# Gated attention: the weighing of the values as three split products

## The chip, the cores and the metric

One core of one Trainium2 chip. The metric is the device time in microseconds of one launch of the whole program, here the median of three runs. Engines: PE (TensorE, matrix products), ACT (ScalarE), DVE (VectorE), POOL (GpSimd), SP (SyncE, issues most transfers).

## The reference

A small transformer of two blocks on 16 sequences of 548 tokens (36 image patches and 512 text tokens) with 128 channels. The change touches one part, the gated attention of the first block, cut here to what matters:

```python
h = x * jax.lax.rsqrt(ms + EPS) * norm_scale
uv = jax.nn.silu(h @ W1 + b1)
u, v, base = jnp.split(uv, [256, 512], axis=-1)
q, k = (base[:, :, None, :] * gamma + beta)[:, :, 0], (...)[:, :, 1]
qk = jnp.einsum('bnd,bmd->bnm', q, k) / 128
qk = _rope(qk)                       # rotates pairs along the m axis
kernel = jnp.square(jax.nn.relu(qk))
out = u * jnp.einsum('bnm,bme->bne', kernel, v)
return out @ W2 + b2 + shortcut
```

The remaining stages (router and experts, spiking attention, last feed-forward) stay as they are. All is float32.

## The kernel before

`gated_attention` works batch by batch (16), tokens in two halves of 274 columns. The inner product with the values sums over 548 keys: two times two tiles of 128, and a tail. It is cut into five units of work, g = 0 to 4: units 0 and 1 are the first half of the queries, 3 and 4 the second, with two of the four 128-key tiles in each, and unit 2 (`TAIL_UNIT`) holds the key tails of both halves.

A unit passes through four engines: PE `score` (products of q and k into PSUM), DVE `rotate` (L704, L705: times cos and sin), POOL `add` (L661, L662, for the tail L659), ACT `kernel_of` (Relu L590, Square L598), PE `weigh` (L509, for the tails L490), which sums over units in the PSUM tile `kv`. After unit 2 and unit 4 DVE's `gate` (L737) multiplies `kv` by u. `down` (L469) is the product with W2 for the batch before, `residual` (L742) adds it to H. Beside that each engine prepares the next batch: POOL `keep_hn` (L635: the rounded tokens) and `make` (L648: q and k), DVE `tokens_low` (L710), `low_of` (L716, L719, L720) and `bias_v` (L728), ACT `base_out`, `u_out`, `v_out` (L563, L569, L576), PE `project_base`, `project_u`, `project_v`.

The scores and the projections are already split products: `split_matmul` multiplies rounded parts (type float32r) and remainders in three matmuls, rounded by rounded, rounded by remainder and remainder by rounded. POOL makes the rounded part, DVE the remainder by a subtraction. `weigh` and `down` use plain float32 matmuls.

The order on each engine is written out by hand in its `units` function, with semaphores between the engines; a queue runs strictly in that order. The tiles of a unit (scores, by_cos, by_sin, rot, kern) have two copies, so unit g waits for unit g - 2 in them. Batch b + 1 is prepared during batch b: on PE, the order in the steady loop is score 2, v tail, weigh 0, score 3, base, weigh 1, down, score 4, weigh 2, u 0, weigh 3, v, score 0 of the next batch, weigh 4, score 1 of the next, u 1.

Of the kernel before, what the change touches and what calls it, by code (L numbers as in the profile page):

```python
# [9 lines left out]
ALU = mybir.AluOpType  # L10
# [331 lines left out]
def gated_attention(nc, k, x, H, HN, moe_d):  # L342
# [7 lines left out]
    with ExitStack() as st:  # L350
# [4 lines left out]
        sin = sb("sin", [P, 3, 2, S])  # L355

        GAP = 32
        hs = [[sb(f"hs{p}{part}", [P, 2, HALF], F32R) for part in range(2)] for p in range(2)]
# [9 lines left out]
        v = [sb(f"v{p}", [P, 5, EXPAND]) for p in range(2)]  # L368
# [18 lines left out]
        v_biased = sem("v_biased")  # L387
# [31 lines left out]
        def _(sp):  # L419
            sp.dma_start(cos[:], x["cos"]).then_inc(tables_in, 16)  # L420
            sp.dma_start(sin[:], x["sin"]).then_inc(tables_in, 16)
# [3 lines left out]
            w = NROWS // 4  # L425
            for sums in (y_d[0], y_d[1]):
                yv = sums.rearrange("(p r) d -> p (r d)", p=P)
                for c in range(4):
                    sp.dma_start(yv[:, c * w:(c + 1) * w], zeros[:]).then_inc(filled, 16)
            sp.dma_start(rows_d[NT:NROWS, :].rearrange("(p r) d -> p (r d)", p=64), zeros[0:64, 0:(NROWS - NT) * ROWW // 64]).then_inc(filled, 16)  # L430
            sp.dma_start(slots_d, x["empty_slots"]).then_inc(filled, 16)
            sp.wait_ge(filled, 16 * 10)

        @block.tensor
        def _(pe):
# [52 lines left out]
            def weigh_tail(p, j):  # L488
                for e in range(2):
                    last = nc.tensor.matmul(kv[:, e, 0:HALF], v[p][0:TAILS, 4, e * P:(e + 1) * P], kern_tail[p][0:TAILS, j, :],  # L490
# [3 lines left out]
            def weigh(b, p, g, first=False):  # L494
                pe.wait_ge(kern_done, UNITS * b + g + 1)
                if g == 0:
                    pe.wait_ge(v_sb, 2 * b + 1)
                    if not first:
                        pe.wait_ge(gated, 2 * b)
                if g == TAIL_UNIT:  # L500
                    pe.wait_ge(v_sb, 2 * b + 2)
                    last = weigh_tail(p, 0)
                else:
                    j, mt = unit(g)
                    if g == TAIL_UNIT + 1:
                        pe.wait_ge(gated, 2 * b + 1)
                    for e in range(2):
                        for side in range(2):
                            last = nc.tensor.matmul(kv[:, e, 0:HALF], v[p][:, mt + 2 * side, e * P:(e + 1) * P],  # L509
                                                    kern[(p + g) % 2][:, side, :], start=mt == 0 and side == 0, stop=False)  # L510
# [3 lines left out]

            def units(b, p, first=False, final=False):
                for g in range(UNITS):
                    if g < 3:
                        score(b, p, g + 2)
                    if g == 0:
                        project_v(b, p, True)  # L520
                    if g == 1 and not final:
                        pe.wait_ge(v_biased, 2 * b + 2)
                        project_base(b + 1, 1 - p)
                    weigh(b, p, g, first)
                    if g == 3 and not final:
                        project_v(b + 1, 1 - p, False)
                    if g >= 3 and not final:
                        score(b + 1, 1 - p, g - 3)
                    if g == 1 and not first:
                        if final:  # L530
                            pe.wait_ge(v_biased, 2 * b + 2)
                        else:
                            pe.wait_ge(base_sb, b + 2)
                        down(b - 1)
                    if g == 2 and not final:
                        if not first:
                            pe.wait_ge(resid, b)
# [2590 lines left out]
```

## Time and profile before

| | us |
|---|---|
| median of 3 runs (1675.97 to 1676.25) | 1676.23 |
| the profiled execution: time | 1674.66 |
| the profiled execution: span | 1672.8 |
| of it the gated attention | about 95 to 458 |
| mean granted clock of TensorE | 0.896 |

| engine | busy us (share of the span) |
|---|---|
| PE | 1300.5 (78%) |
| PE, weight loads | 915.5 (55%) |
| DVE | 1036.9 (62%) |
| ACT | 789.4 (47%) |
| POOL | 875.4 (52%) |

Busy shares are averages over stages with different limits. The stretch from 95 to 458 us is the one that the change touches, and it has to be read on its own. Times in the timeline are microseconds from the start of the span. A matmul's record is longer than the distance to the next one, since matmuls are pipelined: what a group of them costs is the distance between starts. A plain float32 matmul shows as two records. "x8" means eight records merged in one row.

### The profile page before, as it was taken

To read this page: it belongs to the slowest core of one execution; us is meant where nothing else is said; L and a number is where in the kernel's file an instruction comes from. 1 tells how busy PE (TensorE), PEld (TensorE's weight loads), DVE (VectorE), ACT (ScalarE), POOL (GpSimd) and SP (SyncE) were. 2 spreads that over 40 slices of the span, in tenths; PEclk is the share of its full clock that TensorE was granted. 3 is DMA by queue.
4 is the path that set the end of the run, shared out by engine and by line. 5 is a ranking of instruction groups with operands and counts; after the bars stand their busy time and mean duration, and the time that the engine had idled before them with its cause. 6 is when DMAs were issued, how large, how long until landed. Compare 5 with 4: busy or idle time off the path is not lost. (4 is left out here: it accounts for less than half of the span.)

```text
span 1672.8 us, 27218 instructions
## 1 busy us (share of the span) xinstructions
PE 1300.5 (78%) x8667; PEld 915.5 (55%) x8667; DVE 1036.9 (62%) x1943; ACT 789.4 (47%) x1420; POOL 875.4 (52%) x880
## 2 busy tenths in 40 slices
PE   5679999999883430676672883888889888999997
PEld 3567777777652320565561562333333357877775
DVE  2766666666557774211111588888888566667786
ACT  2225454555353330232220454878777657665443
POOL 1455555555331003688885524776776045735766
PEclk8879999999995565899995786999999999999999
DMA  5052000000001031344445200000000311333443
GB/s 181 1 208 114 0 0 0 0 0 0 0 0 28 0 108 28 88 93 83 80 73 154 81 1 2 2 1 0 0 0 1 113 50 55 94 95 46 56 61 40
DMA packets 84627, 81.05 MB, mean 48 GB/s; under 512 B 18330, under 2 KB 73203, under 8 KB 83147
## 3 DMA queue, kind: packets, MB, share of 16 engines
q1 hardware_dynamic: 56205, 59.43, 11.4%
q0 software_dynamic: 26176, 19.40, 8.2%
q10 hardware_dynamic: 2160, 1.13, 0.2%
q8 instruction: 47, 0.77, 0.2%
q14 instruction: 39, 0.31, 0.1%
HBM read 46.36 MB, written 39.64 MB: 51 GB/s over the span
## 5 line engine op out<-in xcount | busy, mean ns | idle before, releaser
L1969 PE MATMUL at_slot<-at_qm,at_ks 128*128 128x512 bf16 (+1 forms) x640 | 160.1, 383 | 19.3 <-DVE at_clip L2174 9.9
L2838 POOL DMA_INDIRECT out_h<-ff_tokens x70 | 109.0, 1557 | 74.7 <-DVE ff_tokens L2891 56.9
L509 PE MATMUL ga_kv<-ga_kern,ga_v 128*128 128x274 f32 x512 | 132.3, 400 | 14.3 <-ACT ga_kern L598 12.8
L2053 ACT ACTIVATE at_clip<-at_slot,at_four 128x1024 bf16<-128x1024 f32 (+1 forms) x96 | 106.8, 1112 | 31.9 <-PE at_slot L1969 30.1
L1452 POOL DMA_INDIRECT moe_sums<-ex_y,slot_sums x69 | 108.3, 1570 | 22.1 <-issue 20.9
L2174 DVE TENSOR_SCALAR at_clip<-at_slot 128x1024 bf16<-128x1024 f32 (+1 forms) x96 | 116.1, 1218 | 3.0 <-PE at_slot L1969 2.6
L509 PEld LDWEIGHTS ga_kv<-ga_kern,ga_v 128*128 128x128 f32 x512 | 92.3, 189 | 37.8 <-ACT ga_kern L598 20.4
L661 POOL TENSOR_TENSOR ga_rot<-ga_by_cos,ga_by_sin 128x274 f32<-128x274 f32 x64 | 48.4, 756 | 114.2 <-DVE ga_by_sin L705 114.1
L590 ACT ACTIVATE ga_rot<-ga_rot 128x274 f32<-128x274 f32 x128 | 55.1, 432 | 109.0 <-POOL ga_rot L661 96.9
L1542 DVE TENSOR_SCALAR ex_share<-ex_rows,owner_sb 128x1 f32<-128x1 f32 x31 | 6.6, 214 | 148.4 <-PE ex_ps_y L1494 148.4
L2828 POOL DMA_INDIRECT by_group<-mx_stage,mx_place_i x69 | 72.0, 1044 | 50.0 <-ACT mx_stage L2714 29.2
L1969 PEld LDWEIGHTS at_slot<-at_qm,at_ks 128*128 128x128 bf16 (+1 forms) x640 | 40.0, 97 | 93.6 <-issue 81.6
L1493 PE MATMUL ex_ps_y<-ex_down,ex_hid 128*128 128x128 f32 (+1 forms) x600 | 86.9, 295 | 3.9 <-ACT ex_hid L1524 3.8
L1436 POOL DMA_INDIRECT ex_rows<-token_rows,slot_tokens x69 | 67.2, 974 | 39.5 <-issue 20.4
L1524 ACT ACTIVATE ex_hid<-ex_ps_up,cols_sb 128x274 f32<-128x274 f32 (+1 forms) x96 | 43.3, 488 | 91.9 <-PE ex_ps_up L1480 91.8
L2110 POOL TENSOR_SCALAR at_qm<-at_qs,at_headmask 128x548 bf16<-128x548 bf16 x120 | 86.3, 738 | 0.0
L1493 PEld LDWEIGHTS ex_ps_y<-ex_down,ex_hid 128*128 128x128 f32 (+1 forms) x600 | 80.6, 204 | 8.2 <-ACT ex_hid L1524 7.0
L1378 POOL DMA_INDIRECT expert_slots<-ct_ids,ct_row x20 | 19.7, 983 | 120.6 <-DVEq L1277 116.0
L2891 DVE SCALAR_TENSOR_TENSOR ff_tokens<-mx_e,ff_tokens 128x128 f32<-128x128 f32 x210 | 72.0, 349 | 15.8 <-ACT ff_tokens L2775 10.8
L2102 POOL TENSOR_SCALAR sa_qkv<-sa_qkv 128x548 f32<-128x548 f32 x48 | 44.5, 927 | 66.5 <-ACT sa_qkv L2065 66.5
L2053 ACT ACTIVATE down_b<-at_slot,at_four 128x1024 bf16<-128x1024 f32 (+1 forms) x48 | 53.4, 1113 | 17.2 <-PE at_slot L1969 16.4
L1518 ACT ACTIVATE ex_xt<-ex_ps_xt 128x256 f32<-128x256 f32 (+1 forms) x32 | 12.7, 396 | 100.6 <-PE ex_ps_xt L1470 100.6
(480 smaller groups left out, 3918.8 us busy)
## 6 DMA issues: line engine op xcount, KB each, us to landing
moe_sums<-ga_zeros SPq DMA_DIRECT2D x8, 1152.0 KB, 13.4
ar_rows<-moe_sums SPq DMA_DIRECT2D x34, 256.0 KB, 3.8
ex_down<-in_down SPq DMA_DIRECT2D x32, 192.0 KB, 2.6
by_group<-in_blank SPq DMA_DIRECT2D x1, 4655.0 KB, 19.8
ff_tokens<-by_group SPq DMA_DIRECT2D x17, 266.0 KB, 3.4
token_rows<-ct_rows SPq DMA_DIRECT2D x17, 256.0 KB, 2.4
out_h<-mx_rows SPq DMA_DIRECT2D x22, 192.0 KB, 2.1
H<-in_text SPq DMA_DIRECT2D x1, 4096.0 KB, 22.1
```

The source lines that it names most:

```text
L509: last = nc.tensor.matmul(kv[:, e, 0:HALF], v[p][:, mt + 2 * side, e * P:(e + 1) * P], kern[(p + g) % 2][:, side, :], start=mt == 0 and si ...
L590: last = nc.scalar.activation(r[:, side], r[:, side], ACT.Relu)
L1436: nc.gpsimd.indirect_dma_start(out=rows[t % NR][:], out_offset=None, in_=rows_d, in_offset=bass.IndirectOffsetOnAxis(ap=gather_idx[:, t:t ...
L1452: nc.gpsimd.indirect_dma_start(out=sums, out_offset=bass.IndirectOffsetOnAxis(ap=scatter_idx[:, t:t + 1], axis=0), in_=y[t % YR][:], in_of ...
L1493: nc.tensor.matmul(out, hid[e % 2][0:m, f, at:at + P], down[e % 2][0:m, f, :], start=opens and f == 0, stop=False)
L1969: last = nc.tensor.matmul(to[r0:r0 + r, g % 2, :].rearrange("p (s n) -> p s n", s=2), ks[m][:, t * P:t * P + r], qm[m][:, 2 * g:2 * g + 2, ...
L2053: nc.scalar.activation(to[0:r], of[0:r], ACT.Relu, bias=four[0:r], scale=-1.0).then_inc(by_act, 1)
L2110: return eng.tensor_scalar(qm[m][:, h, :], qs[:], headmask[:, h:h + 1], 1.0, ALU.mult, ALU.mult)
L2174: nc.vector.tensor_scalar(to[0:r], of[0:r], 4.0, None, ALU.min).then_inc(by_dve, 1)
L2828: nc.gpsimd.indirect_dma_start(out=grouped_d, out_offset=bass.IndirectOffsetOnAxis(ap=place_i[:, t:t + 1], axis=0), in_=stage[:, t, :], in ...
L2838: nc.gpsimd.indirect_dma_start(out=out, out_offset=bass.IndirectOffsetOnAxis(ap=ids, axis=0), in_=R[j % RING], in_offset=None, bounds_chec ...
L2891: nc.vector.scalar_tensor_tensor(r, part(e), share(e), r, ALU.mult, ALU.add).then_inc(acc if e < 3 else weighed, 1)
```

## The change

Kernel and values are each split into a rounded part and a remainder. `v_out` writes its Silu over `v_pre`; POOL rounds it (`round_v`), DVE takes the remainder (`values_low`). ACT squares a unit twice: once into the rounded part of the kernel, once in full precision over `rot`; the remainder is a subtraction, on DVE for units 0 and 4 and on POOL for units 1 and 3 (`kern_low`). PE's `weigh` becomes `weigh_high` (the products with the rounded kernel) and `weigh_low` (those with its remainder), and other groups of products stand between the two in PE's order. In unit 0 the product with the values' remainder is also in `weigh_low`. The tails stay plain float32 and get their own `weigh_tails`. `rot` is now free after the subtraction that reads it.

To make room in SBUF, the zeros from which the expert buffers are filled are a quarter of the width and are sent in 16 transfers per buffer instead of 4, the sine table's tail is a tile of its own, and `ukv` of one half lies over W1.

```diff
-        v = [sb(f"v{p}", [P, 5, EXPAND]) for p in range(2)]
+        v_parts = [[sb(f"v{p}{part}", [P, 4, EXPAND], F32R) for part in range(2)] for p in range(2)]
+        v_tail = [sb(f"v_tail{p}", [2 * GAP, EXPAND]) for p in range(2)]
...
-        kern = [sb(f"kern{p}", [P, 2, HALF]) for p in range(2)]
+        kern_parts = [[sb(f"kern{p}{part}", [P, 2, HALF], F32R) for part in range(2)] for p in range(2)]
...
-        zeros = sb("zeros", [P, NROWS // 4])
+        zeros = sb("zeros", [P, NROWS // 16])
...
-        ukv = [sb(f"ukv{j}", [P, 2, HALF]) for j in range(2)]
+        ukv = [k["W1"][:, 0:S].rearrange("p (e n) -> p e n", e=2), sb("ukv", [P, 2, HALF])]
...
+            def products(p, g, v_part, kern_part, start):
+                j, mt = unit(g)
+                for e in range(2):
+                    for side in range(2):
+                        last = nc.tensor.matmul(kv[:, e, 0:HALF], v_parts[p][v_part][:, mt + 2 * side, e * P:(e + 1) * P],
+                                                kern_parts[(p + g) % 2][kern_part][:, side, :], start=start and side == 0, stop=False)
+                return last
+
+            def weigh_high(b, p, g, first=False):
+                pe.wait_ge(kern_done, UNITS * b + g + 1)
+                if g == 0:
+                    pe.wait_ge(v_rounded, b + 1)
+                    if not first:
+                        pe.wait_ge(gated, 2 * b)
+                if g == TAIL_UNIT + 1:
+                    pe.wait_ge(gated, 2 * b + 1)
+                products(p, g, 0, 0, g in (0, TAIL_UNIT + 1))
+                if g > 0:
+                    products(p, g, 1, 0, False)
+
+            def weigh_low(b, p, g):
+                if g in (0, UNITS - 1):
+                    pe.wait_ge(low_by_dve, 2 * b + 1 + (g > 0))
                 else:
+                    pe.wait_ge(low_by_pool, 2 * b + 1 + (g > 1))
+                last = products(p, g, 0, 1, False)
+                if g == 0:
+                    pe.wait_ge(v_low, b + 1)
+                    last = products(p, g, 1, 0, False)
                 if g == UNITS - 1:
                     last = weigh_tail(p, 1)
                 last.then_inc(kv_done, 1)
...
+                score(b, p, 2)
+                project_v(b, p, True)
+                weigh_high(b, p, 0, first)
+                score(b, p, 3)
+                weigh_low(b, p, 0)
+                pe.wait_ge(v_biased, 2 * b + 2)
+                if not final:
+                    project_base(b + 1, 1 - p)
+                weigh_high(b, p, 1)
+                if not first:
+                    if not final:
+                        pe.wait_ge(base_sb, b + 2)
+                    down(b - 1)
+                weigh_low(b, p, 1)
+                score(b, p, 4)
+                weigh_tails(b, p)
+                if not final:
+                    if not first:
+                        pe.wait_ge(resid, b)
+                    project_u(b + 1, 1 - p, 0)
+                weigh_high(b, p, 3)
+                if not final:
+                    project_v(b + 1, 1 - p, False)
+                weigh_low(b, p, 3)
+                if not final:
+                    score(b + 1, 1 - p, 0)
+                weigh_high(b, p, 4)
+                if not final:
+                    score(b + 1, 1 - p, 1)
+                weigh_low(b, p, 4)
+                if not final:
+                    project_u(b + 1, 1 - p, 1)
...
-                    last = nc.scalar.activation(kern[(p + g) % 2][:], r[:], ACT.Square)
-                last.then_inc(kern_done, 1)
+                    nc.scalar.activation(kern_parts[(p + g) % 2][0][:], r[:], ACT.Square).then_inc(kern_done, 1)
+                    nc.scalar.activation(r[:], r[:], ACT.Square).then_inc(squared, 1)
...
+            def kern_low(b, p, g):
+                pool.wait_ge(squared, 4 * b + g - (g > TAIL_UNIT) + 1)
+                high, low = kern_parts[(p + g) % 2]
+                nc.gpsimd.tensor_tensor(low[:], rot[(p + g) % 2][:], high[:], ALU.subtract).then_inc(low_by_pool, 1)
+
+            def round_v(b, p, first=False):
+                pool.wait_ge(v_sb, 2 * b + 1)
+                if not first:
+                    pool.wait_ge(kv_done, UNITS * b - UNITS)
+                pool.sem_inc(met, 1)
+                nc.gpsimd.tensor_copy(v_parts[p][0][:], v_pre[:]).then_inc(v_rounded, 1)
+
             def units(b, p, first=False, final=False):
                 for g in range(UNITS):
+                    if g in (1, 3):
+                        kern_low(b, p, g)
                     if g < UNITS - 1:
                         add(b, p, g + 1, first and g == 0)
                     elif not final:
                         add(b + 1, 1 - p, 0)
+                        round_v(b + 1, 1 - p, first)
...
+            def values_low(b, p):
+                dve.wait_ge(v_rounded, b + 1)
+                nc.vector.tensor_tensor(v_parts[p][1][:], v_pre[:], v_parts[p][0][:], ALU.subtract).then_inc(v_low, 1)
...
                     if g == 0:
+                        kern_low(b, p, 0)
+                        values_low(b, p)
                         bias_v(b, True, first)
+                    if g == 4:
+                        kern_low(b, p, 4)
```

## Rows read from the trace of the kernel before

**Rows 1.** Busy time by stretch: us, PE, PEld, DVE, ACT, POOL, PEclk, DMA, GB/s

```profile
196.00:238.00 42.00, 40.55 (x219) 33.03 (x219) 28.62 (x42) 21.41 (x38) 22.10 (x31) 1.00 0.00 0
```

**Rows 2.** The page's 40 slices: granted clock of PE in tenths of full speed

```profile
PEclk8879999999995565899995786999999999999999
```

**Rows 3.** Timeline, DVE, first gate of batches 0, 6, 7, 15: start, us, engine, line

```profile
122.58 0.73 DVE L737 TENSOR_TENSOR ga_ukv<-ga_kv,ga_u 128x548 f32<-128x548 f32 x1 [2.75 <-PE ga_kv L490]
...
252.70 0.73 DVE L737 TENSOR_TENSOR ga_ukv<-ga_kv,ga_u 128x548 f32<-128x548 f32 x1 [0.98 <-PE ga_kv L490]
...
274.26 0.73 DVE L737 TENSOR_TENSOR ga_ukv<-ga_kv,ga_u 128x548 f32<-128x548 f32 x1 [0.97 <-PE ga_kv L490]
...
446.09 0.73 DVE L737 TENSOR_TENSOR ga_ukv<-ga_kv,ga_u 128x548 f32<-128x548 f32 x1 [1.08 <-PE ga_kv L490]
```

**Rows 4.** Timeline, PE, batch 6

```profile
240.96 0.30 PE L92 MATMUL ga_scores<-ga_q,ga_k 128*128 128x274 f32 x1
241.09 0.30 PE L93 MATMUL ga_scores<-ga_q,ga_k 128*128 128x274 f32 x1
...
246.92 2.01 PE L509 MATMUL ga_kv<-ga_kern,ga_v 128*128 128x274 f32 x8
248.77 2.01 PE L469 MATMUL ga_misc<-ga_ukv,W_sb 128*128 128x274 f32 x8
...
251.47 1.19 PE L490 MATMUL ga_kv<-ga_kern_tail,ga_v 50*128 50x274 f32 x4
...
258.74 2.12 PE L509 MATMUL ga_kv<-ga_kern,ga_v 128*128 128x274 f32 x8 [0.63 <-ACT ga_kern L598]
```

**Rows 5.** Timeline, DVE, batch 6

```profile
240.46 0.73 DVE L737 TENSOR_TENSOR ga_ukv<-ga_kv,ga_u 128x548 f32<-128x548 f32 x1 [2.35 <-PE ga_kv L490]
241.53 0.73 DVE L704 TENSOR_TENSOR ga_by_cos<-ga_scores,ga_cos 128x548 f32<-128x548 f32 x1 [0.34 <-PE ga_scores L93]
...
245.15 0.73 DVE L710 TENSOR_TENSOR ga_hs<-HN,ga_hs 128x548 fp32r<-128x548 f32 x1 [1.17 <-POOL ga_hs_tail L636]
245.80 0.19 DVE L711 TENSOR_TENSOR ga_hs_tail<-HN,ga_hs_tail 128x36 fp32r<-128x36 f32 x1
245.90 0.71 DVE L698 TENSOR_TENSOR ga_by_cos<-ga_scores,ga_cos 64x548 f32<-64x548 f32 x1
...
253.35 1.15 DVE L716 TENSOR_TENSOR ga_q<-ga_q 128x548 fp32r<-128x548 f32 x1
254.42 0.71 DVE L704 TENSOR_TENSOR ga_by_cos<-ga_scores,ga_cos 128x548 f32<-128x548 f32 x1
...
255.69 0.68 DVE L719 TENSOR_TENSOR ga_k<-ga_k 128x512 fp32r<-128x512 f32 x1
256.29 0.66 DVE L720 TENSOR_TENSOR ga_k_tail<-ga_k,ga_k_tail 128x36 fp32r<-128x36 f32 x1
```

**Rows 6.** Timeline, POOL, batch 6

```profile
244.21 0.64 POOL L635 CAST ga_hs<-HN 128x548 fp32r x1
...
248.22 1.34 POOL L659 TENSOR_TENSOR ga_rot<-ga_by_cos,ga_by_sin 64x548 f32<-64x548 f32 x1 [3.21 <-issue]
...
251.09 0.67 POOL L661 TENSOR_TENSOR ga_rot<-ga_by_cos,ga_by_sin 128x274 f32<-128x274 f32 x1
...
253.91 0.83 POOL L648 TENSOR_SCALAR ga_k_tail<-ga_base,cols_sb 128x36 fp32r<-128x36 f32 x1
255.86 1.04 POOL L661 TENSOR_TENSOR ga_rot<-ga_by_cos,ga_by_sin 128x274 f32<-128x274 f32 x1 [1.11 <-DVE ga_by_sin L705]
```

**Rows 7.** Timeline, ACT, batch 6

```profile
240.13 0.66 ACT L598 ACTIVATE ga_kern<-ga_rot 128x548 f32<-128x548 f32 x1
240.70 1.04 ACT L576 ACTIVATE ga_v<-ga_v_pre 128x1024 f32<-128x1024 f32 x1
242.19 0.72 ACT L569 ACTIVATE ga_u<-ga_misc,cols_sb 128x548 f32<-128x548 f32 x1 [0.45 <-PE ga_misc L93]
```

**Rows 8.** Timeline, PE, unit 4 of the last batch

```profile
450.68 2.12 PE L509 MATMUL ga_kv<-ga_kern,ga_v 128*128 128x274 f32 x8 [1.62 <-ACT ga_kern L598]
```

More of the change, by code:

```diff
@@ L354, in gated_attention @@
         cos = sb("cos", [P, 3, S])
[L355 removed]
+        sin = sb("sin", [P, 2, 2, S])
         GAP = 32
+        sin_tail = sb("sin_tail", [2 * GAP, S])
         hs = [[sb(f"hs{p}{part}", [P, 2, HALF], F32R) for part in range(2)] for p in range(2)]
@@ L513, in weigh, with weigh_tails @@
                 last.then_inc(kv_done, 1)
+            def weigh_tails(b, p):
+                pe.wait_ge(kern_done, UNITS * b + TAIL_UNIT + 1)
+                pe.wait_ge(v_sb, 2 * b + 2)
+                weigh_tail(p, 0).then_inc(kv_done, 1)
             def units(b, p, first=False, final=False):
[L516 to L537, printed above, removed]
-                        project_u(b + 1, 1 - p, 0)
-                    if g == 4 and not final:
-                        project_u(b + 1, 1 - p, 1)
@@ L653, in add @@
                 pool.wait_ge(rot_done, n + 1)
-                if not first:
+                if g == 0 and not first:
+                    pool.wait_ge(low_by_pool, 2 * b)
+                if g == 1 and not first:
+                    pool.wait_ge(low_by_dve, 2 * b)
+                if g == 3:
+                    pool.wait_ge(low_by_pool, 2 * b + 1)
+                if g == 2:
+                    pool.wait_ge(low_by_dve, 2 * b + 1)
+                if g == 4:
                     pool.wait_ge(kern_done, n - 1)
@@ L680, in _ @@
             add(0, 0, 0, True)
+            round_v(0, 0, True)
             units(0, 0, first=True)
@@ L698, in rotate @@
                     nc.vector.tensor_tensor(by_cos[par][0:2 * GAP], xs[0:2 * GAP], halves(cos[0:2 * GAP, 2, :]), ALU.mult)
-                    nc.vector.tensor_tensor(by_sin[par][high], xs[low], halves(sin[low, 2, 0, :]), ALU.mult)
-                    nc.vector.tensor_tensor(by_sin[par][low], xs[high], halves(sin[high, 2, 1, :]), ALU.mult).then_inc(rot_done, 1)
+                    nc.vector.tensor_tensor(by_sin[par][high], xs[low], halves(sin_tail[low]), ALU.mult)
+                    nc.vector.tensor_tensor(by_sin[par][low], xs[high], halves(sin_tail[high]), ALU.mult).then_inc(rot_done, 1)
                 else:
@@ L724, in bias_v @@
                 dve.wait_ge(v_ps, 2 * b + tails + 1)
-                if not first:
+                if tails and not first:
                     dve.wait_ge(v_sb, 2 * b)
@@ L737, in gate, with kern_low @@
                 nc.vector.tensor_tensor(ukv[j][:], kv[:, :, 0:HALF], u[p][:, :, j, :], ALU.mult).then_inc(gated, 1)
+            def kern_low(b, p, g):
+                dve.wait_ge(squared, 4 * b + g - (g > TAIL_UNIT) + 1)
+                high, low = kern_parts[(p + g) % 2]
+                nc.vector.tensor_tensor(low[:], rot[(p + g) % 2][:], high[:], ALU.subtract).then_inc(low_by_dve, 1)
+            def values_low(b, p):
+                dve.wait_ge(v_rounded, b + 1)
+                nc.vector.tensor_tensor(v_parts[p][1][:], v_pre[:], v_parts[p][0][:], ALU.subtract).then_inc(v_low, 1)
             def residual(b):
```

41 lines of the change are left out of this document (17 added, 24 removed).

## The prediction, made before the changed kernel had run

> **What bounds the kernel now.** I read the busy times by stretch first [rows 1]. In 42 us of the gated attention PE is busy 40.55 us at a granted clock of 1.00, DVE 28.62 and POOL 22.10. That says PE, but a busy sum hides pipelining, so I went to the timeline. The gate of a batch's first half starts at 252.70 and again at 274.26 [rows 3]: one batch takes 21.56 us, and the attention is 16 of these.
>
> PE's own order comes next [rows 4]. Split products (fp32r) are issued every 0.13 us (240.96, 241.09), a score's six take 0.76 us, and 0.31 us after the last slot (241.22) DVE starts on them (241.53 [rows 5]). A plain f32 weigh unit of four products holds PE from 246.92 to 248.77, 1.85 us. The tail's two hold it from 251.47 until their gate starts at 252.70, 1.23 us, with 0.08 in front 1.31. One real stall stands in the batch: weigh unit 4 starts at 258.74, 0.63 us late, released by ACT's Square. So the kernel is bound by PE, with the chain gate, low_of, rotate 4, add 4, Square just behind it.
>
> Last, the other three engines [rows 5 to 7], because the change puts all its new work there. What the reader is to see is who waits for whom between DVE and POOL. A DVE subtraction with both inputs in SBUF takes 0.73 us when POOL is idle (245.15, 548 columns), but 1.15 at 253.35, beside POOL's tensor_scalars. The 36-column L720 takes 0.66 at 256.29 against 0.19 for its twin L711. POOL's add takes 1.04 at 255.86 instead of 0.67: 256.90 less 0.67 is 256.23, just 0.54 after L719 began. POOL's 36-column k_tail takes 0.83. So these instructions run one after the other, not side by side, and a waiting one gets its turn between two instructions of the other engine. DVE instructions that read PSUM show no such stretch: L704 at 254.42 takes 0.71 beside k_tail, 0.73 at 241.53 with POOL idle.
>
> **The change part by part.** PE: per batch 16 plain products (4 units of 1.85 us, 7.40 us) become 48 split ones of 0.127 us, 6.10 us: 1.3 us less. The tails stay. The stall at unit 4 and small gaps are the most that could go on top.
>
> ACT: a second Square per unit, 4 per batch. A Square holds ACT 0.57 us (240.13 to 240.70 [rows 7]), 2.3 us more on an engine that is half idle; it matters because v_out and u_out queue behind it.
>
> POOL gets kern_low of units 1 and 3 and round_v. A 548-column tensor_tensor is 1.34 us (L659 [rows 6]), a cast of 548 columns 0.64, so 1024 columns about 1.20: 3.9 us. DVE gets kern_low of units 0 and 4 and values_low. L719's 512 columns held the pair 0.54 us, so 548 columns 0.57 and 1024 columns 1.07: 2.2 us, and by the rows above these are lost to POOL too wherever it has work.
>
> Other edits at nothing: the zero fill as 32 transfers of a quarter of the size on SP's queue, whose last wait comes at the end of a block with over 300 us of cover, and costs SP alone without it; the tables as four transfers and the smaller memset, behind which DVE waits for PE's first scores anyway; the aliased ukv and sin_tail, with the same instructions as before.
>
> The new waits: round_v waits for v_out (ACT), and behind it in POOL's queue stand add 1, keep_hn and all later work, for which ACT and PE wait. values_low waits for round_v, and behind it on DVE stand bias_v of the tail, tokens_low and rotate 2, for which PE's base projection, score 4 and POOL wait. PE's low products wait for kern_low, and v's projection and the next scores stand behind them. So I laid one batch out, each engine's queue in program order, with durations from the rows. Time 0 is where the previous batch's second gate starts (240.46 in the trace of now).
>
> Rotate 0 of the new batch ends at -3.1. kern_low 4 of the old batch (DVE) and add 0 (POOL, two halves, 1.28) meet, and add 0 ends at -1.2, 0.57 later than alone. From the end of an add to a high product PE needs 1.21 us now (add 4 ends 0.63 after 256.90, PE starts at 258.74), of which the Square is 0.66, so Square starts 0.50 after an add. ACT: two Squares and v_out (1.04), to 1.5. POOL: round_v to 2.7. DVE: gate to 0.65, rotate 1 to 2.0, kern_low 0, held by round_v, 2.7 to 3.3. POOL's add 1 has its first half to 3.9; DVE's values_low to 5.0; the second half to 5.6; keep_hn to 6.4. DVE: tokens_low 6.5 to 7.2, rotate 2. That one and its handover take 2.32 us (245.90 to add 2 at 248.22), so POOL's add 2 starts at 9.6 (now 7.8) and ends at 10.9. Up to here 1.8 us are lost.
>
> From there POOL: make q 1.54, to 12.4; add 3, to 13.7. ACT: 0.50, two Squares, u_out 0 (0.72), to 16.1; PE projects v (12 products, 1.43) to 17.6. In parallel POOL: make k (1.54) with low_of q let in between, to 15.8, k_tail 16.1, kern_low 3 to 17.4; then DVE's low_of k, in turn with add 4, to 18.6. PE's next score 0 waits for that: 18.7 to 19.5; rotate 0 begins 0.31 later and takes 1.36, to 21.1. It ended at -3.1 one batch earlier: 24.2 us a batch. By the other branch: add 4 17.9 to 19.2, high products from 20.4, 1.02, the score 0.76, low products 0.51, tail 1.31: 24.0. I take 24.0, since every contest was charged in full.
>
> Sum: from the first batch's first gate to the last's are 446.09 - 122.58 = 323.5 us, 15 x 21.57 [rows 3]. 15 x (24.0 - 21.57) = 36.5 us. The first batch pays round_v and its follow-up once more, about 1.5 us. The last has no next batch to feed, and its unit 4, 1.62 us late by Square at 450.68 [rows 8], can hide its own low part: 0. Together 38 us. The profiled execution took 1674.7 us with a span of 1672.8, 1.5 below the median of 1676.2; by the span the new profile shows 1711, and the median becomes 1714.
>
> What the trace of before does not show is the new DVE work beside POOL. Its bounds are 0 (as for DVE's instructions on PSUM) and its full hold plus the wait. I take the latter: these have the form of L716 and L719 (f32 less fp32r into fp32r), the nearest rows. With 0 the path is: v_out to 1.1, round_v 2.3, add 1 3.6, keep_hn 4.4, tokens_low and rotate 2, add 2 from 7.5, add 3 to 11.65; Squares and u_out 2.4, v 1.43, low products 0.51, score 0, 0.31 and rotate 0 2.4, to 18.45: 21.5 us a batch.
>
> The Trainium skill, SBUF — State Buffer, section "SBUF: two separate sides", has this as a rule that speaks against the change: VectorE instructions with two SBUF inputs and GpSimd instructions that read SBUF take one port pair as an exclusive lock for the whole instruction, and the loser fully blocks. By the rule the result is the 24 us batch, without it the 21.5 us one. The trace agrees with it in the stretched instructions [rows 5 and 6].
>
> **The rivals.** (A) PE sets the batch, which gets shorter. For: PE is the busiest now. From the tails' start to the high products of unit 4 are 7.3 us now, at least 6.9 with add 4 not stretched; then PE needs 3.6 us to the end of the tail and 9.15 back to the tails (seven groups of six 0.76 or less, high and low products 3.1, down 1.85, base in them): 19.7 to 20.0 us, and 15 x (19.85 - 21.57) = -26 gives 1650 us. It decides if v_out, round_v and kern_low 3 find slack in POOL's queue. Against: even without contention POOL's path is 21.5. (B) The path through POOL and ACT binds, but its contests are absorbed: 21.5 us a batch, 1677 us. Against: the 1.04 and 1.15 us rows. (C) Between: one or two contests fall into idle time (kern_low 4 after add 0, low_of k before kern_low 3): 22.1 to 23.3 us a batch, 1685 to 1704 us. (D) Worse: PE's longer idle stretches cost it granted clock, which is 9 tenths or more of full in the attention's slices but 5 or 6 tenths in slices of other stages [rows 2]; 25 us a batch or more, 1730 and up. (E) The new products are not single passes: the scores' products of the same shape and type run at 0.127 us, so this gets nothing of its own.
>
> **How the numbers follow.** Forecast (23.3 to 24.8 us a batch, 1704 to 1727): 0.50. C: 0.20. D: 0.08. B: 0.10, 0.06 of it within the bound and 0.04 above it. A: 0.12. That makes faster 0.12, same 0.06, slower 0.82, at a bound of 0.2% (3.4 us), about what a measurement of this kernel can tell from no change. The range leaves out A and D, together 0.20: from B's 1677 to the forecast's 1727.
>
> **What would show it.** First gates 24 us apart (A: 20, B: 21.5). PE well under 40.55 us busy in 42. The new 548-column subtractions on DVE at 1.0 us or more in the mean against 0.73 alone, POOL's adds well above 0.67. PE idle before the base projection (released by tokens_low), before score 0 (by low_of k), before the high products of units 0 and 4. Add 2 some 9.6 us after the second gate. I am wrong if PE idles under 1 us per batch, or if the new subtractions keep to 0.73 us beside a busy POOL.

## The result and the profile after

The changed kernel takes 1729.7 us (median of 4, 1726.67 to 1729.99) against 1676.1 us: ratio 1.0316, 95% interval 1.0298 to 1.0334. It is slower, as forecast, by 53.6 us where 38 were forecast, and 2.7 us beyond the end of the range. The profiled execution took 1730.0 us with a span of 1728.2.

The first gates again, DVE's timeline of the changed kernel, batches 0, 5, 6 and 15 (of before: rows 3):

```profile
124.70 0.73 DVE L791 TENSOR_TENSOR W_sb<-ga_kv,ga_u 128x548 f32<-128x548 f32 x1 [2.76 <-PE ga_kv L496]
...
249.32 0.73 DVE L791 TENSOR_TENSOR W_sb<-ga_kv,ga_u 128x548 f32<-128x548 f32 x1 [1.50 <-PE ga_kv L496]
...
274.17 0.73 DVE L791 TENSOR_TENSOR W_sb<-ga_kv,ga_u 128x548 f32<-128x548 f32 x1 [1.47 <-PE ga_kv L496]
...
497.40 0.73 DVE L791 TENSOR_TENSOR W_sb<-ga_kv,ga_u 128x548 f32<-128x548 f32 x1 [1.87 <-PE ga_kv L496]
```

A batch takes 274.17 - 249.32 = 24.85 us. The fifteen distances are 497.40 - 124.70 = 372.7 us against 323.5: 49.2 of the 55.4 us by which the span grew. The first gate comes 2.1 us later, the last batch takes 1.4 us more from its first gate to its residual (497.40 to 509.64 against 446.09 to 456.95), and 2.7 us lie behind the attention.

Busy time by stretch, changed kernel (columns as in rows 1):

```profile
196.00:238.00 42.00, 34.77 (x218) 29.25 (x217) 30.91 (x40) 22.53 (x40) 27.50 (x33) 1.00 0.00 0
...
498.00:502.00 4.00, 2.51 (x13) 2.22 (x13) 1.41 (x3) 1.59 (x5) 2.66 (x3) 0.63 0.00 0
502.00:506.00 4.00, 4.00 (x15) 3.58 (x16) 0.73 (x1) 0.49 (x1) 0.00 (x0) 0.52 0.00 0
```

PE is busy 34.77 us in 42 where it was 40.55, at full clock; DVE has 2.3 and POOL 5.4 us more. No engine is full: the batch is a chain. From the first gate on, only the last batch shows a lower granted clock, 0.50 from 499 to about 506 us, the lower of the two levels (1.2 of 2.4 GHz). PE in that batch:

```profile
498.28 2.50 PE L504 MATMUL ga_kv<-ga_kern,ga_v 128*128 128x274 f32 x12 [0.91 <-DVE W_sb L791]
501.99 3.11 PE L504 MATMUL ga_kv<-ga_kern,ga_v 128*128 128x274 f32 x12 [1.21 <-ACT ga_kern L628]
505.03 1.57 PE L496 MATMUL ga_kv<-ga_kern_tail,ga_v_tail 50*128 50x274 f32 x4
```

The twelve products of unit 4 take 3.0 us (501.99 to 505.03), where twelve at 0.127 us take 1.5. What made the clock fall is not shown: PE had waited 0.91 us just before, and in the kernel before it waited 0.91 and 1.62 us in the last batch (446.97, and 450.68 in rows 8) and kept 1.00.

Who waits, from the waits of the changed kernel between 130 and 480 us, some 14 batches (waiting instruction, releaser, us in total, times, longest):

```profile
PE ga_misc L91 <- DVE ga_hs_tail L765: 19.7, 14, 1.4
PE ga_scores L91 <- DVE ga_k_tail L774: 18.0, 15, 1.2
PE ga_misc L91 <- ACT ga_u L599: 12.1, 14, 0.9
PE ga_kv L504 <- DVE ga_kern L796: 5.6, 14, 0.4
```

PE waits 1.4 us a batch for tokens_low before the base projection, 1.2 for low_of k before score 0, 0.9 for u_out before the values' tail, and 0.4 for kern_low 4 before the low products of unit 4. The first two places are those of the prediction; the other two it did not have, and the wait before the high products of unit 4 that it had is not there. PE from score 0 on, in the same batch:

```profile
255.00 0.39 PE L91 MATMUL ga_scores<-ga_q,ga_k 128*128 128x274 f32 x1 [1.21 <-DVE ga_k_tail L774]
...
255.86 1.18 PE L504 MATMUL ga_kv<-ga_kern,ga_v 128*128 128x274 f32 x8
256.87 0.29 PE L91 MATMUL ga_scores<-ga_q,ga_k 128*128 128x274 f32 x1
...
258.21 0.79 PE L504 MATMUL ga_kv<-ga_kern,ga_v 128*128 128x274 f32 x4 [0.42 <-DVE ga_kern L796]
```

Now DVE and POOL around them, one batch:

```profile
251.91 2.85 DVE L773 TENSOR_TENSOR ga_k<-ga_k 128x512 fp32r<-128x512 f32 x1
254.68 0.18 DVE L774 TENSOR_TENSOR ga_k_tail<-ga_k,ga_k_tail 128x36 fp32r<-128x36 f32 x1
...
257.44 0.72 DVE L796 TENSOR_TENSOR ga_kern<-ga_rot,ga_kern 128x548 fp32r<-128x548 f32 x1
260.15 0.73 DVE L791 TENSOR_TENSOR ga_ukv<-ga_kv,ga_u 128x548 f32<-128x548 f32 x1 [2.00 <-PE ga_kv L496]
...
262.07 0.72 DVE L796 TENSOR_TENSOR ga_kern<-ga_rot,ga_kern 128x548 fp32r<-128x548 f32 x1
263.72 1.68 DVE L800 TENSOR_TENSOR ga_v<-ga_v_pre,ga_v 128x1024 fp32r<-128x1024 f32 x1 [0.93 <-POOL ga_v L712]
```

```profile
251.59 1.36 POOL L705 TENSOR_TENSOR ga_kern<-ga_rot,ga_kern 128x548 fp32r<-128x548 f32 x1
252.92 0.66 POOL L699 TENSOR_TENSOR ga_rot<-ga_by_cos,ga_by_sin 128x274 f32<-128x274 f32 x1
253.54 0.66 POOL L700 TENSOR_TENSOR ga_rot<-ga_by_cos,ga_by_sin 128x274 f32<-128x274 f32 x1
257.60 1.09 POOL L699 TENSOR_TENSOR ga_rot<-ga_by_cos,ga_by_sin 128x274 f32<-128x274 f32 x1 [3.39 <-DVE ga_by_sin L759]
...
262.25 1.44 POOL L712 CAST ga_v<-ga_v_pre 128x1024 fp32r<-128x1024 f32 x1 [2.94 <-ACT ga_v_pre L604]
263.65 0.67 POOL L699 TENSOR_TENSOR ga_rot<-ga_by_cos,ga_by_sin 128x274 f32<-128x274 f32 x1
264.28 1.65 POOL L700 TENSOR_TENSOR ga_rot<-ga_by_cos,ga_by_sin 128x274 f32<-128x274 f32 x1
...
269.88 1.34 POOL L697 TENSOR_TENSOR ga_rot<-ga_by_cos,ga_by_sin 64x548 f32<-64x548 f32 x1 [0.80 <-DVE ga_by_sin L754]
```

Three meetings are to be seen. At 257.44 kern_low 4 runs 0.72 us undisturbed and add 0 waits for it, 1.09 instead of 0.66. At 263.72 values_low waits for the first half of add 1, runs, and the second half takes 1.65. And low_of k (L773, 512 columns, 0.68 us in rows 5) takes 2.85 us: it starts to wait in kern_low 3 and is let in only when POOL's queue is empty, behind kern_low 3 and both halves of add 4 (254.16).

### The profile page after: what moved, and what is told of

It is laid out like the page before. It is cut to its first block and busy times, and to the rows that moved or that the text cites. A ratio compares the mean times of both kernels' runs of the same rounds, so it can differ in the third digit from the quotient of the medians.

```text
span 1728.2 us, 28002 instructions
## 1 busy us (share of the span) xinstructions
PE 1297.9 (75%) x8923; PEld 927.7 (54%) x8923; DVE 1100.1 (64%) x1991; ACT 821.2 (48%) x1484; POOL 957.7 (55%) x928
## 5 line engine op out<-in xcount | busy, mean ns | idle before, releaser
L2036 PE MATMUL at_slot<-at_qm,at_ks 128*128 128x512 bf16 (+1 forms) x640 | 160.4, 384 | 19.6 <-DVE at_clip L2241 10.0
L504 PEld LDWEIGHTS ga_kv<-ga_kern,ga_v 128*128 128x128 f32 x768 | 108.2, 194 | 33.5 <-ACT ga_kern L628 10.4
L1445 POOL DMA_INDIRECT expert_slots<-ct_ids,ct_row x20 | 19.7, 984 | 120.7 <-DVEq L1344 116.2
```

The lines of the kernel that those rows point to most:

```text
L504: last = nc.tensor.matmul(kv[:, e, 0:HALF], v_parts[p][v_part][:, mt + 2 * side, e * P:(e + 1) * P], kern_parts[(p + g) % 2][kern_part][:, ...
L2036: last = nc.tensor.matmul(to[r0:r0 + r, g % 2, :].rearrange("p (s n) -> p s n", s=2), ks[m][:, t * P:t * P + r], qm[m][:, 2 * g:2 * g + 2, ...
```

## The experiments

All versions start from the changed kernel unless said otherwise. "Batch" is the distance of first gates, last less first, over 15. The ratios are to the kernel before on the same chip. The chip of e1 to e4 took 1759.2 us for the kernel before, where the others took 1675 to 1676, so for these four the batch is the number to compare. The kernel before has no trace on that chip: its 21.57 us are those of the first one.

| run | batch, us | total, us | ratio to before (interval) |
|---|---|---|---|
| before | 21.57 | 1676.1 | 1 |
| changed | 24.85 | 1729.7 | 1.0316 (1.0298 to 1.0334) |
| e1 PE's work only | 21.03 | 1753.8 | 0.9974 (0.9960 to 0.9988) |
| e2 no subtraction on DVE | 23.03 | 1784.3 | 1.0140 (1.0117 to 1.0163) |
| e3 values rounded by ACT | 23.83 | 1797.3 | 1.0206 (1.0183 to 1.0229) |
| e4 values_low from PSUM | 23.86 | 1800.0 | 1.0225 (1.0206 to 1.0244) |
| changed, again | 24.84 | 1729.7 | 1.0321 (1.0301 to 1.0342) |
| e5 POOL yields to low_of k | 23.75 | 1714.7 | 1.0220 (1.0194 to 1.0246) |
| e6 all kern_low on DVE | 24.49 | 1724.9 | 1.0288 (1.0265 to 1.0311) |
| e7 e6 and e3 | 23.83 | 1715.8 | 1.0226 (1.0202 to 1.0250) |
| e8 early tokens | - | 1728.5 | 1.0325 (1.0304 to 1.0346) |
| e12 early tokens, again | 24.72 | 1725.6 | 1.0300 (1.0279 to 1.0320) |
| e9 before, early tokens | 21.10 | 1669.1 | 0.9968 (0.9954 to 0.9983) |
| e10 e8, e5 and ACT rounds | 23.11 | 1705.2 | 1.0183 (1.0166 to 1.0199) |
| e11 e1, early tokens | 20.21 | 1656.5 | 0.9891 (0.9874 to 0.9907) |
| e13 e8, kern_low 1 later | 24.95 | 1732.8 | 1.0338 (1.0321 to 1.0355) |
| e14 e10, kern_low 1 later | 23.31 | 1713.5 | 1.0234 (1.0217 to 1.0251) |
| e15 rounded product only | 18.90 | 1636.5 | 0.9769 (0.9753 to 0.9786) |

In some runs single batches have a lower granted clock in the mean, 0.93, and take 0.4 to 1.6 us longer (2.2 us in e15, at 0.84); they are in the column "batch". Leaving out the first and the last of the fifteen distances and those at a lower clock, a batch takes 24.9 us in the changed kernel, 24.6 in e12, 24.9 in e13, 23.5 in e7, 22.8 in e10 and 23.1 in e14. In e10 the clock is 0.50, the lower level, from about 269.5 to 272.9 us, soon after PE had waited 1.6 us for Square, and that batch takes 24.40 us. The same wait stands in every batch of e10, and only three of the thirteen in the middle show the fall. The first batch has 0.92 to 0.95 in e1 to e4 and one more 0.93 in e3; all others of e1 to e6, e9 and e11 have full clock.

The repeated run was expected so:

> The changed kernel once more, on the chip of the other runs of this call, so that they have it beside them. Every theory expects the 24.85 us per batch of its first profile, 3.2% above the kernel before.

It gave 24.84 us.

**PE's side alone.** The new products stay, their remainders are tiles of zeros set once:

```diff
-                    nc.scalar.activation(r[:], r[:], ACT.Square).then_inc(squared, 1)
...
-                    last = nc.scalar.activation(v_pre[:], v_pre[:], ACT.Silu)
+                    last = nc.scalar.activation(v_parts[p][0][:], v_pre[:], ACT.Silu)
...
-                    if g in (1, 3):
-                        kern_low(b, p, g)
...
-                        round_v(b + 1, 1 - p, first)
...
-                        kern_low(b, p, 0)
-                        values_low(b, p)
```

> PE's side of the change alone: the new products in their new order, but the remainders of kernel and values stay tiles of zeros that are set once; ACT writes the rounded parts itself (one Square per unit, one Silu for the values), so the second Square, round_v, kern_low and values_low are left out. Theory T (PE's work is shorter, what makes the kernel slower is the added work in the queues of POOL, DVE and ACT): the batch is PE's own, 19.7 to 20.0 us against 21.57 before and 24.85 changed, total near 1650 us (1646 to 1656). Rival R1 (the split products and their order on PE do not bring it, through weight loads or switches between them): 21.5 us a batch or more, total 1675 or above.

21.03 us: below before, so PE's new products do bring time (R1 falls), and the 3.8 us up to 24.85 come with the work on the other three engines. But it is 1.0 us above my 19.7 to 20.0. PE's timeline shows what I had left out of that path:

```profile
213.00 1.28 PE L504 MATMUL ga_kv<-ga_kern,ga_v 128*128 128x274 f32 x8 [0.52 <-ACT ga_kern L625]
...
221.87 0.40 PE L91 MATMUL ga_misc<-ga_hs,ga_W 128*128 128x274 f32 x1 [0.62 <-DVE ga_hs_tail L749]
```

PE has become early enough for the base projection to wait for tokens_low, which follows gate, rotate 1, add 1 and keep_hn. I tested that by doing keep_hn and tokens_low one batch earlier, in idle time of POOL and DVE before add 0 and the second gate:

```diff
-                    if g == 0 and not final:
-                        keep_hn(b + 1, 1 - p, first)
...
+                        if not last:
+                            keep_hn(b + 2, p)
                         add(b + 1, 1 - p, 0)
...
-                    if g == 0 and not final:
-                        tokens_low(b + 1, 1 - p)
+                    if g == 4 and not final and not last:
+                        tokens_low(b + 2, p)
```

> The kernel of the first run of PE's work alone (remainders left out, tiles of zeros in their place) with the early tokens. Theory T3 (its 21.03 us instead of the 19.7 to 20.0 expected are PE's wait for tokens_low before base, 0.62 us a batch, and the rest of that stretch): 20.2 to 20.6 us a batch, 0.8 to 1.2% below the kernel before. Rival R1 (its products cost more than their 0.127 us): 20.9 us or more.

20.21 us, within the expectation, and PE's wait for tokens_low is gone. So 0.8 us of e1's shortfall was this wait; 0.2 us above my 20.0 are left.

**Which of the added work.** First without DVE's part (the low parts of units 0 and 4 and of the values are left out, and PE's waits for them):

```diff
-                        kern_low(b, p, 0)
-                        values_low(b, p)
                         bias_v(b, True, first)
-                    if g == 4:
-                        kern_low(b, p, 4)
```

> The changed kernel without the three subtractions on DVE (kern_low of units 0 and 4 and values_low are left out, the tiles keep zeros or old values); the second Squares on ACT and kern_low 1, 3 and round_v on POOL stay. Theory T (POOL and DVE take turns, so DVE's subtractions delay POOL's adds): POOL's add 1 and add 0 go back to 0.67 us for each half, add 2 starts 1.3 us earlier against the second gate, and a batch is 22.9 to 23.4 us, total 1699 to 1708. Rival R2 (only POOL's own longer queue counts, DVE's subtractions run beside it): at most 0.3 us less per batch, 24.5 us or more, total 1724 or above. low_of k should stay at 2.9 us, since kern_low 3 and add 4 still stand back to back on POOL.

23.03 us, as T expected. All halves of the adds are back at 0.67 us, the second of add 1 among them (of the changed kernel: 1.65):

```profile
228.34 1.04 POOL L709 CAST ga_v<-ga_v_pre 128x1024 fp32r<-128x1024 f32 x1 [2.93 <-ACT ga_v_pre L601]
229.33 0.67 POOL L696 TENSOR_TENSOR ga_rot<-ga_by_cos,ga_by_sin 128x274 f32<-128x274 f32 x1
229.96 0.67 POOL L697 TENSOR_TENSOR ga_rot<-ga_by_cos,ga_by_sin 128x274 f32<-128x274 f32 x1
```

low_of k stays at 2.94 us, as expected too. Then the sharper test, the same instruction on DVE at the same place with one input from PSUM (the remainders of the values are then not computed):

```diff
-                nc.vector.tensor_tensor(v_parts[p][1][:], v_pre[:], v_parts[p][0][:], ALU.subtract).then_inc(v_low, 1)
+                dve.wait_ge(v_ps, 2 * b + 2)
+                nc.vector.tensor_tensor(v_parts[p][1][:], misc[:].rearrange("p b (s n) -> p (b s) n", s=2), v_parts[p][0][:], ALU.subtract).then_inc(v_low, 1)
```

> values_low reads its first input from PSUM (the tile misc, whatever stands there) instead of v_pre in SBUF: the same instruction, engine, place and number of columns, but only one input in SBUF, so the values' remainders are wrong numbers. Theory T (it is the two SBUF inputs that make DVE and POOL take turns): values_low falls from 1.68 to about 1.2 us, the second half of POOL's add 1 from 1.65 to 0.67, a batch is 23.7 to 24.1 us, total 1712 to 1719. Rival R2 (no exclusion between them; the long records have another cause, as ACT's Squares or the column count): the two records and the batch stay, total 1729.

DVE and POOL:

```profile
212.43 1.23 DVE L801 TENSOR_TENSOR ga_v<-ga_misc,ga_v 128x1024 fp32r<-128x1024 f32 x1 [0.93 <-POOL ga_v L712]
```

```profile
212.37 0.67 POOL L699 TENSOR_TENSOR ga_rot<-ga_by_cos,ga_by_sin 128x274 f32<-128x274 f32 x1
212.99 0.68 POOL L700 TENSOR_TENSOR ga_rot<-ga_by_cos,ga_by_sin 128x274 f32<-128x274 f32 x1
```

The two run side by side, 1.68 becomes 1.23, 1.65 becomes 0.68, and the batch 23.86 us. So one instruction's turn with POOL costs 1.0 us a batch here, and it is the second SBUF input that makes it take turns (R2 falls).

**The rounding moved to ACT** (a second Silu, v_pre into the rounded part, round_v dropped):

```diff
+                    nc.scalar.activation(v_parts[p][0][:], v_pre[:], ACT.Silu).then_inc(v_rounded, 1)
                     last = nc.scalar.activation(v_pre[:], v_pre[:], ACT.Silu)
...
-                        round_v(b + 1, 1 - p, first)
```

> The rounded values are written by ACT with a second Silu (0.95 us more on ACT) instead of by POOL's cast (round_v, 1.44 us). Theory T (the path v_out, round_v, add 1, keep_hn, tokens_low, rotate 2, add 2 sets the batch): add 2 comes about 0.9 us earlier, a batch is 23.8 to 24.1 us, total 1714 to 1719. Rival R3 (the batch is set elsewhere, as by low_of k before score 0 alone, or by ACT, which the second Silu loads further): 24.8 us or more, total 1729 or above.

23.83 us, as T expected: POOL's path from v_out to add 1 is on what sets the batch.

**low_of k's wait.** One more wait makes a gap in POOL's queue:

```diff
+                if g == UNITS - 1 and not final:
+                    pool.wait_ge(qk_low, 2 * b + 4)
```

> The changed kernel with one more wait: POOL waits for low_of k (DVE) before add 4, so its queue has a gap behind kern_low 3. Theory T2 (low_of k takes 2.9 us because DVE gets no turn while POOL's kern_low 3 and the two halves of add 4 stand back to back; it could have run after kern_low 3, as I had assumed in the prediction): low_of k falls to 1.5 to 1.9 us, PE's 1.2 us wait for it before score 0 shrinks below 0.3 us, add 4 comes 0.8 us later, and a batch is 23.9 to 24.4 us. Rival R4 (the wait before score 0 does not set the batch, another path is as long): low_of k falls as well, but the batch stays at 24.7 us or more, or grows by add 4's delay.

DVE's low_of k and POOL's add 4 now:

```profile
271.52 1.59 DVE L775 TENSOR_TENSOR ga_k<-ga_k 128x512 fp32r<-128x512 f32 x1
```

```profile
271.21 1.35 POOL L707 TENSOR_TENSOR ga_kern<-ga_rot,ga_kern 128x548 fp32r<-128x548 f32 x1
273.44 0.67 POOL L701 TENSOR_TENSOR ga_rot<-ga_by_cos,ga_by_sin 128x274 f32<-128x274 f32 x1 [0.88 <-DVE ga_k_tail L776]
```

and PE's high products of unit 4:

```profile
275.95 1.29 PE L504 MATMUL ga_kv<-ga_kern,ga_v 128*128 128x274 f32 x8 [1.57 <-ACT ga_kern L628]
```

low_of k falls to 1.6 us, PE's wait before score 0 is gone from the list of its waits, and the batch is 23.75 us, a little below the 23.9 to 24.4 expected. What sets the batch has changed: PE now waits 1.6 us for Square before the high products of unit 4, behind the delayed add 4. The gain of 1.1 us is not that of low_of k's turn alone, since round_v no longer meets kern_low 0 and takes 1.04 us instead of 1.44. Next kern_low 1 and 3 off POOL:

```diff
-                    if g in (1, 3):
-                        kern_low(b, p, g)
...
-                    if g == 4:
-                        kern_low(b, p, 4)
+                    if g in (1, 3, 4):
+                        kern_low(b, p, g)
```

> All four kern_low on DVE, none on POOL: each holds the pair for 0.57 us instead of 1.33 us. Theory T: nothing stands between make k and add 4 on POOL, low_of k ends about 1 us earlier against the second gate, a batch is 23.7 to 24.3 us. Rival R2 (POOL and DVE do not get in each other's way, DVE's queue is simply long): DVE has 1.2 us more per batch in front of the same rotates, a batch is 24.85 us or more.

24.49 us, between the two, so T missed: low_of k is down to 1.16 us, but kern_low 1 now stands on DVE before rotate 3 and runs beside add 2, which takes 1.74 us instead of 1.34, and both halves of add 4 are stretched. With ACT's rounding as well:

> All four kern_low on DVE and the rounding of the values by ACT's second Silu: POOL has none of the change's new work, all remainders are computed. Theory T (the losses on the two shared stretches add up): a batch is 22.7 to 23.2 us, 1.0 to 1.4% above the kernel before. Rival R5 (with POOL's load gone the wait for the shared stretch was not the point, and the remainders themselves cost nothing): 21.6 us or less, no slower than before.

23.83 us, a miss: ACT's two Silus push u_out, for which PE's projection of the values' tail waits up to 1.8 us, and seven of the fifteen batches have a granted clock of 0.93. Those in the middle at full clock take 23.5 us, still more than T's 23.2. Neither T nor R5.

**The repairs.** Early tokens in the changed kernel:

> The changed kernel with keep_hn (POOL) and tokens_low (DVE) done one batch earlier, at the end of the batch before, where POOL and DVE are idle: add 1, keep_hn, tokens_low no longer stand in front of the base projection and of rotate 2. Theory T (the stretch from the second gate to add 2 is on the path that sets the batch): PE's 1.4 us wait before the base projection goes, and add 2 starts 0.8 us earlier (kern_low 1 now stands in front of it), a batch is 23.6 to 24.2 us. Rival R6 (only the stretch from make k to score 0 sets the batch): 24.7 us or more.

No gain in the times, so I was wrong. It was run once more for its trace:

> The changed kernel with the early tokens once more, for its trace. It was not faster than the changed kernel by its times. Theory T4 (the batch is a closed path through POOL: add 1, Square, kern_low 1, add 2; taking tokens_low out only lets kern_low 1, which waits for the second Square and stands before add 2, take its place, and the moved work now meets add 0): a batch is 24.6 to 25.0 us, kern_low 1 starts right after the second Square, add 2 directly behind it, and one half of add 0 takes over 1 us. Rival R8 (the move made PE late somewhere): a wait of over 1 us a batch on PE that the changed kernel does not have.

24.72 us. What T of the run before had named does happen: PE's wait before the base projection is gone, and add 2 starts 9.0 us after the second gate instead of 9.7. At full clock a batch takes 24.6 us instead of 24.9, so the move brings 0.3 us; six of the fifteen batches have a granted clock of 0.93, which takes most of that back. kern_low 1 does stand directly before add 2. But the larger part of the loss is elsewhere: low_of k takes 3.5 us now, as keep_hn has lengthened the row of instructions behind which it waits, and PE waits 1.8 us before score 0 instead of 1.2.

```profile
225.02 3.51 DVE L776 TENSOR_TENSOR ga_k<-ga_k 128x512 fp32r<-128x512 f32 x1
```

```profile
224.79 1.36 POOL L705 TENSOR_TENSOR ga_kern<-ga_rot,ga_kern 128x548 fp32r<-128x548 f32 x1
226.11 0.66 POOL L699 TENSOR_TENSOR ga_rot<-ga_by_cos,ga_by_sin 128x274 f32<-128x274 f32 x1
226.74 0.66 POOL L700 TENSOR_TENSOR ga_rot<-ga_by_cos,ga_by_sin 128x274 f32<-128x274 f32 x1
227.35 0.63 POOL L665 CAST ga_hs<-HN 128x548 fp32r x1
227.93 0.67 POOL L666 CAST ga_hs_tail<-HN 128x36 fp32r x1
```

It is let in after the cast that ends at 227.98, the fourth of POOL's instructions since it began to wait. kern_low 1 behind add 2:

> The early tokens, and kern_low 1 behind add 2 in POOL's queue instead of before it. Theory T4: add 2 no longer waits for the second Square and rotate 2 alone releases it, but make q and all behind it stand behind kern_low 1 as before, so POOL's work from add 2 to add 4 starts about 1 us earlier: a batch is 23.6 to 24.3 us. Rival R4 (the path from add 2 to add 4 is not what sets the batch): 24.6 us or more.

24.95 us, and at full clock 24.9 against e12's 24.6, so 0.3 us are lost: add 2 starts 1.0 us earlier, but kern_low 1 behind it lets make q start no earlier than before, and low_of k still takes 3.5 us. T4 falls as far as it puts the loss on kern_low 1. The three repairs together (early tokens, yielding, ACT's rounding with u_out between the two Silus), and the same with kern_low 1 behind add 2:

> The changed kernel with all three repairs: early tokens, POOL's wait for low_of k before add 4, and the values rounded by ACT's first Silu, with u_out between it and the second. All remainders are computed. Theory T (each removes its loss): a batch is 21.7 to 22.4 us, 0.2 to 0.8% above the kernel before. Rival R7 (DVE is full then, at 16 us of work and its turns with POOL): 22.8 us or more.

> The version with all three repairs, and kern_low 1 behind add 2. All remainders are computed. It had 23.1 us a batch with kern_low 1 before add 2. Theory T4: 22.0 to 22.7 us a batch. Rival R7 (the turns of DVE and POOL at add 0 and at values_low and low_of k set it): no change, 22.9 us or more.

23.11 and 23.31 us, both above what T and T4 expected; e10 is the best that I had with all remainders computed, still 1.8% slower than before. Against the changed kernel, e5 and e3 gained 1.1 and 1.0 us and the early tokens 0.3 at full clock. Together they would give 22.5 us from 24.9; e10 has 22.8 at full clock, and three batches at the lower clock bring its mean to 23.11. What is left: PE's wait of 1.6 us for Square before the high products of unit 4 came with e5's yield and stays, and tokens_low (1.19 us) and add 0 (its second half 1.16) meet now. kern_low 1 behind add 2 costs 0.3 us here too.

**Faster than both.** The early tokens in the kernel before:

> The kernel before with the same move of keep_hn and tokens_low. Theory T: before was bound by PE with weigh 4 late by the chain tails, gate, low_of, rotate 4, add 4, Square, which the move does not shorten, so a batch is 21.3 to 21.6 us, total 0 to 4 us less. Rival R6 as an opposite (tokens_low's stretch set the batch before too): 21.0 us or less, 8 us less or more.

21.10 us and 6.0 us less in all, 0.47 us a batch, more than the 0 to 0.3 that T's 21.3 to 21.6 us allowed. A wait of PE for the tokens is not the reason: in the list of waits of the kernel before its products have none, and its weight loads 1.2 us in 14 batches. The first gate and low_of q, and PE's high products of unit 4, in e9:

```profile
249.37 0.73 DVE L740 TENSOR_TENSOR ga_ukv<-ga_kv,ga_u 128x548 f32<-128x548 f32 x1 [0.98 <-PE ga_kv L490]
250.01 0.72 DVE L719 TENSOR_TENSOR ga_q<-ga_q 128x548 fp32r<-128x548 f32 x1
```

```profile
254.98 2.12 PE L509 MATMUL ga_kv<-ga_kern,ga_v 128*128 128x274 f32 x8 [0.45 <-ACT ga_kern L598]
```

Unit 4 starts 5.61 us after the first gate, where it was 6.04 (252.70 to 258.74), and from there to the next first gate nothing has changed (15.5 us in both). With the tokens out of the way, rotate 2, add 2 and make k come earlier, make k ends just before the gate, and low_of q takes 0.72 us in every batch where it took 1.15 to 1.26 beside make k. So the chain that T had named was shortened, by one meeting less of DVE and POOL. It computes everything that the kernel before computes, and it beats both. And with only the product of the rounded parts (both products with remainders are left out):

> Early tokens, and only the product of the rounded parts (a third of the new products; the two products with remainders are left out, the sum stays in the same numbers as with tiles of zeros). PE has 4.1 us less work per batch than the version with zeros, which had 20.2 us a batch. Theory T5 (the chain gate, low_of, rotate 4, add 4, Square, high products, tail and gate is then what sets the batch, PE waits in it): a batch is 18.6 to 19.8 us. Rival R9 (PE's work is still what counts): 16.1 to 17 us.

18.90 us: with 4.1 us of products taken away, 1.3 us come back, and PE waits for u_out (1.1 us), Square (0.6) and low_of k (0.5). The batch is T5's, and PE's work alone no longer sets it; but the longest wait, for u_out, was not in T5's chain.

## Why the prediction was nearly right, and where it was not

Right: that the kernel gets slower, by the turns of DVE and POOL and the longer path v_out, round_v, add 1, keep_hn, tokens_low, rotate 2, add 2, make, low_of, score 0. Counted from the second gate (235.22 and 260.15), add 0 ends at -0.8 (forecast -1.2), v_out at 1.9 (1.5), add 1 at 5.8 (5.6), add 2 starts at 9.7 (9.6), add 4 ends at 19.0 (19.2). e2, e3 and e4 took away one link each and hit their expected 23 to 24 us.

The step that failed is one sentence: "then DVE's low_of k, in turn with add 4, to 18.6". I had assumed, from the waits of before, that a waiting DVE instruction gets its turn between two instructions of POOL. It did not: low_of k with its tail ended at 19.6, score 0 began at 19.8 (18.7), and the batch took 24.85 us. e5 and e12 show that the length of low_of k follows POOL's queue, from both sides: with a gap in it 1.6 us, with more instructions behind 3.5. How this one microsecond reaches the gate: behind score 0 stand rotate 0 and kern_low 4 on DVE, and PE's low products of unit 4 wait 0.4 us for kern_low 4. The gate comes 5.3 us after low_of k's end (254.86 to 260.15). 18.6 + 5.3 are 23.9 us, just under the 24.0 of my other branch; 19.6 + 5.3 are 24.9, the batch as measured.

So the 24.0 was right for the layout, but not for my reason. The 24.2 beside it takes rotate 0 to end 3.1 us before the second gate. No row shows that: it was 2.35 before and is 2.6 now (257.52 to 260.15).

```profile
237.39 0.72 DVE L705 TENSOR_TENSOR ga_by_sin<-ga_scores,ga_sin 128x548 f32<-128x548 f32 x1
```

Of the span's growth 17.4 us were missed (55.4 less 38; in the median 15.6): 12.7 in the fifteen batches (49.2 less 36.5), and 0.6 in the first batch, 2.1 us instead of 1.5. Another 1.4 are in the last batch, which I had put at 0, and 2.7 lie behind the attention, which was not in the sum. The last batch's 1.4 us are the twelve products of unit 4 at the lower clock (3.0 us instead of 1.5): rival D, in one batch of 16. What the 2.7 us are was not looked into.

Wrong as well: the sign that I named for the new subtractions, 1.0 us or more on DVE. The two kern_low there keep to a median of 0.72 us, beside a busy POOL, which I had named as a sign that I am wrong. It was a bad sign, not a failed mechanism: DVE had asked first, and the price stood on POOL (1.09, 1.44, 1.65). Only values_low and low_of k showed it on DVE.

Two readings of the prediction are off without changing its result. The list behind rival A's 9.15 us says seven groups of six products; that time holds five of 0.76 us and one of three. And the slice of rows 2 in which the attention begins shows 7 tenths of the clock, not 9.

Rival A's 19.7 to 20.0 us was too low by the wait for tokens_low, for the most part, as e1 (21.03) and e11 (20.21) show; by e1's batch its price was -8 us rather than -26. Rival B's mechanism is excluded by e4. The rule of the Trainium skill, SBUF — State Buffer, section "SBUF: two separate sides", held where I had leaned on it: with one input in PSUM the exclusion is gone (1.65 to 0.68 us). For two instructions that meet it says that the one which starts first has the ports; for one that has been waiting while the other engine's next stands ready it names no order, and that was the missing number.

## What to carry to other kernels

A change that shortens the busiest engine by moving work to others has to be priced on the chain through their queues: here 1.3 us of products less per batch, of which 0.5 reached the batch in e1, was paid with 3.8 us on POOL, DVE and ACT. Count an elementwise instruction with two SBUF inputs on DVE as occupying POOL too, and look at what stands back to back in POOL's queue when DVE asks: a queue without a gap can hold a short DVE instruction for its whole length, and a deliberate wait can pay (e5). When variants are compared by the mean of a loop, look at the granted clock of each pass first: in e10 three passes at the lower level hid a third of a microsecond. Work without a dependence on the current step (here the next tokens) belongs in an idle stretch, but a repair at one place puts its instruction in front of somebody elsewhere; only the run shows the sum.

## What the runs showed of the hardware that I had not expected

A waiting DVE instruction is not always served at POOL's next instruction boundary. values_low and L720 got in between the two halves of an add, and so did low_of k in e6 (1.16 us); but low_of k, which began to wait in kern_low 3, was passed over at two boundaries in every batch of the changed kernel from the first gate on (2.84 to 2.94 us), and in e12 at three in eleven batches (3.49 to 3.52 us) and at two in another three (2.95 us, and the cast behind takes 1.11):

```profile
200.55 2.95 DVE L776 TENSOR_TENSOR ga_k<-ga_k 128x512 fp32r<-128x512 f32 x1
```

```profile
200.31 1.36 POOL L705 TENSOR_TENSOR ga_kern<-ga_rot,ga_kern 128x548 fp32r<-128x548 f32 x1
...
202.88 1.11 POOL L665 CAST ga_hs<-HN 128x548 fp32r x1
```

In these three the instructions and their order are the same as in the eleven, and low_of k begins to wait as long after kern_low 3's start (0.23 to 0.24 us in both). So neither the kind of POOL's instructions nor, to a hundredth of a microsecond, the moment at which DVE asks decides it alone. What does is open.

POOL's cast of 1024 columns takes 1.04 us alone (e2), not the 1.20 that I had scaled up from 548 columns. And the new split products cost what the scores' did: eight take 1.01 us (255.86 to 256.87), 0.126 each.
